# Graph network, sort and counts: bucket counts by summed signs, destination degrees counted inside the steps, half of the flag scatters behind the sort

## The reference

```python
h = relu(layernorm(x))
for _ in range(4):                     # STEPS
    msg = einsum('eij,ej->ei', (attr @ W_bond + b_bond).reshape(-1, 32, 32), h[dst])
    agg = segment_sum(msg, src)
    h = gru_cell(agg, h)
x = x + h
h = relu(layernorm(x))
deg = segment_sum(ones, dst)           # how many edges each node receives
dis = where(deg > 0, rsqrt(deg), 0)
out = x + segment_sum(h[src] * dis[src] * weight * dis[dst], dst)
```

## Time and profile before

| | us |
|---|---|
| median of 3 runs | 27753.59 (27752.26 to 27754.51) |
| the profiled execution, whole | 27758.91 |
| its span in the profile | 27757.1 |
| counting | 50 to 732 |
| placement | 757 to 4832 |
| layout | 4832 to 4876 |
| the four steps | 4876 to 22680 |

### The profile page before, as it was taken

The page is one execution under the profiler, slowest core; times in us unless marked ns, Lnnn a source line. Parts: engine busy times, 40 slices in busy tenths (PEclk is TensorE's granted clock), DMA queues, the critical chain, the costliest instruction groups (busy, mean ns, idle before and its releaser), DMA issues. The chain is left out here.

```text
span 27757.1 us, 248614 instructions
## 1 busy us (share of the span) xinstructions
PE 12374.2 (45%) x67675; PEld 9367.5 (34%) x67676; DVE 9831.1 (35%) x17524; ACT 4931.9 (18%) x12149; POOL 19766.5 (71%) x20823
## 2 busy tenths in 40 slices
PE   5566665455555455555455555545555530000004
PEld 5344443333333333333333333333333320000004
DVE  9899998222222222222222222222222230000007
ACT  7333333111111111111111111111111110000004
POOL 0677777777777677777677777767777767777771
PEclk8777777777777677777677777767777765555555
DMA  4233332111111111111111111111111111121113
GB/s 168 84 94 94 94 94 79 30 29 28 28 28 29 26 29 28 28 29 28 26 28 28 28 29 28 27 27 28 29 28 28 28 33 45 44 46 44 44 42 90
DMA packets 1814377, 1246.48 MB, mean 45 GB/s; under 512 B 1182629, under 2 KB 1744754, under 8 KB 1789679
## 3 DMA queue, kind: packets, MB, share of 16 engines
q1 hardware_dynamic: 583936, 850.03, 10.1%
q0 software_dynamic: 666016, 324.92, 8.0%
q10 hardware_dynamic: 564300, 70.11, 1.7%
HBM read 957.69 MB, written 285.80 MB: 45 GB/s over the span
## 5 line engine op out<-in xcount | busy, mean ns | idle before, releaser
L1083 POOL DMA_INDIRECT h_rows<-h_table,rec x13680 | 12910.7, 944 | 4284.0 <-issue 4118.8
L1233 PE MATMUL outer<-a_masked,h_by_quarter 128*128 128x136 f32 x27360 | 5316.2, 370 | 8726.5 <-DVE h_by_quarter L1124 8726.5
L1233 PEld LDWEIGHTS outer<-a_masked,h_by_quarter 128*128 128x128 f32 x27360 | 5045.0, 272 | 9193.2 <-issue 9193.2
L1279 ACT COPY outer_sums<-outer 128x408 f32<-128x408 f32 x4560 | 2276.2, 499 | 14770.2 <-PE outer L1233 14271.9
L1124 DVE TENSOR_TENSOR h_by_quarter<-h_rows,gates 128x1920 f32<-128x1920 f32 x912 | 1964.6, 2154 | 7011.0 <-DMA h_rows<-h_table,rec 7011.0
L1510 POOL DMA_INDIRECT messages_by_bucket<-ms,ix x3420 | 3279.1, 959 | 1063.5 <-issue 1042.4
L855 POOL DMA_INDIRECT edges_by_node<-row,place x3125 | 2992.9, 958 | 952.8 <-issue 945.2
L1117 DVE TENSOR_TENSOR a_masked<-rec,gates 128x2040 f32<-128x2040 f32 x912 | 2071.0, 2271 | 4308.7 <-PE outer L1233 4288.1
L1209 PE MATMUL msg_psum<-outer_sums,w_bond_blocks 128*128 128x480 f32 x7752 | 3521.2, 601 | 0.0
L1209 PEld LDWEIGHTS msg_psum<-outer_sums,w_bond_blocks 128*128 128x128 f32 x7752 | 1583.2, 215 | 1400.5 <-issue 1400.5
L1492 PE MATMUL pgb<-ident_f,gsp_by_chunk_of_tile 128*120 128x128 f32 x228 | 61.6, 426 | 3848.1 <-DVE gsp_by_chunk_of_tile L1430 3848.1
(11 more groups left out here) (277 smaller groups left out, 12593.5 us busy)
## 6 DMA issues: line engine op xcount, KB each, us to landing
h_rows<-h_table,rec POOLq DMA_INDIRECT x13680, 2.4
key_row<-source_keys SPq DMA_DIRECT2D x125, 1600.0 KB
rec<-edges_by_node SPq DMA_DIRECT2D x1140, 157.5 KB, 2.2
low_key_row<-source_low_keys SPq DMA_DIRECT2D x126, 800.0 KB
carry_flags<-carry_flags SPq DMA_DIRECT2D x285, 240.0 KB
mr<-messages_by_bucket SPq DMA_DIRECT2D x220, 264.0 KB, 2.7
messages_by_bucket<-zeros SPq DMA_DIRECT2D x36, 1600.0 KB, 37.0
chunk_sums<-scan_t ACTq DMA_DIRECT2D x912, 60.0 KB
```

The lines of the kernel that those rows point to most:

```text
L1083: pool.indirect_dma_start(out=hb[j][:, u, :], out_offset=None, in_=ht, in_offset=bass.IndirectOffsetOnAxis(ap=rec[j][:, u, W_DST:W_DST + 1 ...
L1233: last = pe.matmul(pt[(j * NB + g) % RING][:, at:at + KC], hq[j % 2][:, u, :, :].rearrange("p q d -> p (q d)"), am[j % 2][:, u, :, :].rear ...
L1279: act.copy(ts[b][:, :, at:at + w].rearrange("p k (u c) -> p u k c", c=CPT), pt[(j * NB + g) % RING][:, 0:GPB * KC].rearrange("p (u k c) -> ...
```

## The change

- Counting: DVE builds only `oh_s` and `oh_hs`, with keys that ACT has copied twice over once for all iterations (`lo_s2`, `hi_s2`). PE makes one product for each tile. The destination bucket counts come from ACT: 97 passes over all 3125 high keys of a partition, each giving sign(hi - h + 0.5) and its sum over the row (`accum_out`). Half the difference of two neighbouring sums is the count of a bucket in a partition, and the plan sums over partitions as before.
- Steps: in each group from the third on (55 of 57, 220 in all) DVE copies 15 tiles of destination keys into PSUM (`take_dst`), builds their onehots (`onehots_of_dst`), PE multiplies them in 15 products into `px` (`count_dst`), and DVE adds the result to `node_d`, which is cleared ahead of the steps. The keys `lo_d`, `hi_d` stay in SBUF for that.
- Flags: 49 of the 98 flag scatters stay ahead of the placement, 49 go into the layout block, where the wait for all of them is too.

```diff
+JD = 15
...
+    CS = NGR - 2
+    KI = up(STEPS * CS * JD, J1) // J1
+    assert STEPS * CS * JD >= T1 and KI > IT1
...
+        lo_d = sb("lo_d", [P, KI, J1], BF16)
+        hi_d = sb("hi_d", [P, KI, J1], BF16)
...
+                lo_s2 = sb("lo_s_twice", [P, IT1, J1, 2], BF16)
+                hi_s2 = sb("hi_s_twice", [P, IT1, J1, 2], BF16)
+                signs = [sb(f"signs{k}", [P, IT1, J1], BF16) for k in range(4)]
+                above = sb("above_bucket", [P, P])
+                nsign = sb("sign_sums", [P, HB + 1])
...
-                    ch(dve.tensor_scalar(half_below[:], iota_f[:], -0.5, None, ALU.add))
+                    ch(dve.tensor_scalar(above[:], iota_f[:], -1.0, 0.5, ALU.mult, ALU.add))
+                    ch(dve.memset(nsign[:, 0:1], float(T1)))
+                    ch(dve.memset(nsign[:, HB:HB + 1], -float(T1)))
...
+                    dve.wait_ge(s_key, 1)
+
                     def build(it, b, i):
                         dve.wait_ge(s_cnt, it + 1)
-                        dve.wait_ge(s_key, it + 1)
-                        for k, out_ in enumerate((oh_s, oh_hs, oh_d)):
-                            onehots(dve, out_[b][:], iota_b, key_v[b][:, k])
-                        last = onehots(dve, oh_hd[b][:], iota_b, key_v[b][:, 3, 0:JV])
-                        last.then_inc(s_oh_v, 1)
+                        onehots(dve, oh_s[b][:], iota_b, lo_s2[:, bass.ds(it, 1)].rearrange("p a u k -> p (a u) k"))
+                        onehots(dve, oh_hs[b][:], iota_b, hi_s2[:, bass.ds(it, 1)].rearrange("p a u k -> p (a u) k")).then_inc(s_oh_v, 1)
                     pairs(dve, IT1, build)
                     dve.wait_ge(s_cnt, IT1 + 2)
                     ch(dve.tensor_copy(node_s[:, 0:HB], pnode_s[:, 0:HB]))
-                    ch(dve.tensor_copy(ncode[:], pcode_d[:, 0:HB + 1]))
-                    ch(dve.tensor_tensor(node_d[:, 0:HB], ncode[:, 1:HB + 1], ncode[:, 0:HB], ALU.subtract))
-                    ch(dve.scalar_tensor_tensor(out=node_d[:, 0:HB], in0=node_d[:, 0:HB], scalar=0.5, in1=pnode_d[:, 0:HB],
-                                                op0=ALU.mult, op1=ALU.add))
+                    dve.wait_ge(s_sign, HB - 1)
+                    ch(dve.tensor_tensor(node_d[:, 0:HB], nsign[:, 0:HB], nsign[:, 1:HB + 1], ALU.subtract))
+                    ch(dve.tensor_scalar(node_d[:, 0:HB], node_d[:, 0:HB], 0.5, None, ALU.mult))
...
+                    act.wait_ge(s_split, 1)
+                    act.copy(lo_s2[:], lo_s[:, 0:IT1].unsqueeze(3).broadcast_to([P, IT1, J1, 2]))
+                    act.copy(hi_s2[:], hi_s[:, 0:IT1].unsqueeze(3).broadcast_to([P, IT1, J1, 2])).then_inc(s_key, 1)
                     act.wait_ge(s_split, 2)
-
-                    def build(it, b, i):
-                        act.wait_ge(s_cnt, it + 1)
-                        for k, key in enumerate((lo_s, hi_s, lo_d, hi_d)):
-                            last = act.copy(key_v[b][:, k], twice(of(key, it)))
-                        last.then_inc(s_key, 1)
-                        act.mul(neg[b][:], of(hi_d, it), -1.0).then_inc(s_neg, 1)
-                        act.wait_ge(s_neg, it + 1)
-                        for u in range(JC):
-                            last = act.activation(code_hd[b][:, u, :], half_below[:, 0:HB + 1], ACT.Sign, bias=neg[b][:, JV + u:JV + u + 1], scale=1.0)
-                        last.then_inc(s_code, 1)
-                    pairs(act, IT1, build)
+                    for h in range(1, HB):
+                        if h > 4:
+                            act.wait_ge(s_sign, h - 4)
+                        act.activation(signs[h % 4][:], hi_d[:, 0:IT1], ACT.Sign, bias=above[:, h:h + 1], scale=1.0,
+                                       accum_out=nsign[:, h:h + 1]).then_inc(s_sign, 1)
...
                     def count(it, b, i):
                         pe.wait_ge(s_oh_v, it + 1)
-                        pe.wait_ge(s_code, it + 1)
                         for u in range(J1):
-                            pe.matmul(pnode_s[:, 0:HB], oh_s[b][:, u, :], oh_hs[b][:, u, :], start=False, stop=False, skip_group_check=True)
-                            if u < JV:
-                                pe.matmul(pnode_d[:, 0:HB], oh_d[b][:, u, :], oh_hd[b][:, u, :], start=False, stop=False, skip_group_check=True)
-                            else:
-                                last = pe.matmul(pcode_d[:, 0:HB + 1], oh_d[b][:, u, :], code_hd[b][:, u - JV, :], start=False, stop=False,
-                                                 skip_group_check=True)
+                            last = pe.matmul(pnode_s[:, 0:HB], oh_s[b][:, u, :], oh_hs[b][:, u, :], start=False, stop=False, skip_group_check=True)
                         last.then_inc(s_cnt, 1)
...
-                    for h in range(HB):
-                        pool.indirect_dma_start(
-                            out=flags, out_offset=bass.IndirectOffsetOnAxis(ap=flag_at[:, h:h + 1], axis=0),
-                            in_=zrow[:], in_offset=None, bounds_check=NCH - 1, oob_is_err=False).then_inc(s_flag, 16)
+                    def clear_flags(columns):
+                        for h in columns:
+                            pool.indirect_dma_start(
+                                out=flags, out_offset=bass.IndirectOffsetOnAxis(ap=flag_at[:, h:h + 1], axis=0),
+                                in_=zrow[:], in_offset=None, bounds_check=NCH - 1, oob_is_err=False).then_inc(s_flag, 16)
+                    clear_flags(range(HB // 2))
...
-                    pool.wait_ge(s_flag, 16 * HB)
...
+                @block.gpsimd
+                def _(pool):
+                    for h in range(HB // 2, HB):
+                        pool.indirect_dma_start(
+                            out=flags, out_offset=bass.IndirectOffsetOnAxis(ap=flag_at[:, h:h + 1], axis=0),
+                            in_=zrow[:], in_offset=None, bounds_check=NCH - 1, oob_is_err=False).then_inc(s_flag, 16)
+                    pool.wait_ge(s_flag, 16 * HB)
...
+                dst_ps = pg[:, GB, CPT + NQ:CPT + NQ + 2 * JD]
+                o_dl = sb("dst_low_onehots", [P, JD, P], BF16)
+                o_dh = sb("dst_bucket_onehots", [P, JD, HB], BF16)
+                lo_all = lo_d[:].rearrange("p i u -> p (i u)")
+                hi_all = hi_d[:].rearrange("p i u -> p (i u)")
...
+                        def take_dst(g):
+                            tiles = bass.ds(s * (CS * JD) + (g - 2) * JD, JD)
+                            dve.wait_ge(s_do, s * CS + g - 1)
+                            dve.tensor_copy(dst_ps[:, 0:JD], lo_all[:, tiles])
+                            dve.tensor_copy(dst_ps[:, JD:2 * JD], hi_all[:, tiles]).then_inc(s_dk, 1)
+
+                        def onehots_of_dst(g):
+                            dve.wait_ge(s_dk, s * CS + g - 1)
+                            dve.wait_ge(s_dc, s * CS + g - 1)
+                            dve.tensor_tensor(o_dl[:], iota_b[:].unsqueeze(1).broadcast_to([P, JD, P]),
+                                              dst_ps[:, 0:JD].unsqueeze(2).broadcast_to([P, JD, P]), ALU.is_equal)
+                            dve.tensor_tensor(o_dh[:], iota_b[:, 0:HB].unsqueeze(1).broadcast_to([P, JD, HB]),
+                                              dst_ps[:, JD:2 * JD].unsqueeze(2).broadcast_to([P, JD, HB]), ALU.is_equal).then_inc(s_do, 1)
+
+                        def add_degrees(g):
+                            dve.wait_ge(s_dc, s * CS + g)
+                            dve.wait_ge(s_dd, s * CS + g - 1)
+                            dve.tensor_tensor(node_d[:, 0:HB], node_d[:, 0:HB], px[:, 0, 0:HB], ALU.add).then_inc(s_dd, 1)
+
                         def group(n0, ng, b, i, g, past, last=False):
                             if past == 2:
                                 scan(ng - 2, b, s * USES[b] + i - 1)
+                                take_dst(g)
                             for j in range(GI):
                                 if j + 1 < GI:
                                     make_a(n0 + j + 1, ng, j + 1, (j + 1) % 2)
+                                if past == 2 and j == 2:
+                                    add_degrees(g)
                                 spread_h(n0 + j, ng, j)
+                                if past == 2 and j == 0:
+                                    onehots_of_dst(g)
...
+                        def count_dst(ng, g_):
+                            pe.wait_ge(s_do, s * CS + g_)
+                            pe.wait_ge(s_sc, ng + 1)
+                            hold(pe)
+                            for u in range(JD):
+                                last = pe.matmul(px[:, 0, 0:HB], o_dl[:, u, :], o_dh[:, u, :], start=(u == 0), stop=(u == JD - 1))
+                            last.then_inc(s_dc, 1)
...
                                         weigh(ng - 1, 1 - b, n0 * NB + RING, j)
                                     if g == WEIGH_AT and j == 2 and past == 2:
```

(48 more changed lines are left out.)

2 lines of the change are left out of this document (removed).

## The result

| | us |
|---|---|
| before, median of 4 runs | 27754.05 |
| changed, median of 4 runs | 27436.11 (27435.28 to 27437.25) |
| ratio | 0.9886, 95% interval 0.9868 to 0.9903 |
| difference | -317.9; forecast -320.6 (27433) |

The account below looks back on a forecast made before the run. DVE was taken to bound the counting, POOL everything from placement to messages. Terms -294.6 - 57.3 + 32.0 + 0.2 = -319.7 us gave 27439.2 profiled, forecast 27433 us, range 27415 to 27500.

Parts of the forecast that it names:

- The counting: Counting block: DVE keeps only two onehots, 3.09 us an iteration in place of 5.45; ends at 437.7, -294.6 us.
- The rival that register addresses halve DVE's pace: Counting block: onehots reading keys at a register address take 6.3 us an iteration, +404, 27837 us; chance 0.03.
- that of ACT as the bound: Counting block: ACT's passes at 5.8 us each would set its end, 27608 us in all; chance 0.03.
- The flags ahead: Ahead of the placement: 49 flag scatters instead of 98 bring the first row scatter to 825.5, -57.3 us.
- Places first, flags second: Placement's start: with 49 flags POOL is through at 820.2, before the first places; the first row scatter goes at 825.5.
- The layout block: Layout block: 49 flags make POOL its bound, lasting 76.3 us in place of 44.3, +32.0 us.
- the meeting: Layout block: flag scatters held beside DVE's three wide products and a few copies, taken as +10 us.
- The steps: Steps: 990 us of added DVE work and 15 PE products a group hide beside POOL's gathers, cost 0.
- The slack itself: Steps: gather 9 after a group's second tile has 2.95 us to spare after three PE batches; the count takes 1.2.
- Sum: Whole kernel: -294.6 - 57.3 + 32.0 + 0.2 = -319.7 us; profiled 27758.9 becomes 27439.2, less 5.3 gives 27433.

Follow-up runs that it names:

- three and four times: Changed kernel with each group's 15 degree products made three times: 33908.20 us; four times: 34195.23 (kernel before 33510.48), again 34164.88 (before 33477.75).

## Why the prediction was right

**The counting, -294.6 forecast, -295.0 measured.** The mechanism held, and the sizes nearly: start 50.16 (50.0), 3.08 us an iteration over all 125 (3.09), 2.31 us behind the last onehot (1.7), end 437.5 (437.7). The last two erred by 1 us and 0.6 against each other. ACT's pass is 2.89 us and 0.19 for the sum, started 2.88 us apart (3.05 taken), so it ends at 329 and not at 346, which costs nothing. The rival that register addresses halve DVE's pace is out (1.83 us for 3200 elements, as before), and so is that of ACT as the bound.

**The flags ahead, -57.3 forecast, -56.8 measured.** The places were ready 67.6 us behind the first flag, as before; the first row scatter came 0.8 us after them, where I had taken 0.2. Places first, flags second was the right order on this chip; the runs on another show that it is this chip's: there the places move with the flags.

**The layout block, +32.0 forecast, +34.0 measured.** The meeting was sized right: the first scatter starts at 4480.28 and the last at 4551.25, 70.97 us for 48 distances of 1.275 = 61.2, so 9.8 us for the meeting against 10 taken. That it fits so well is in part luck. I had three products hold POOL for about 3.3 us each; the square took only 2.2 us from it, since the scatter beside it began 1.1 us late, and the third took 4.3, since its scatter was held by the `tensor_scalar` behind the product too, of which I had not thought. What was mis-sized is the ends: 0.7 us until POOL starts, and 5.7 us behind the last scatter where I took 3.8 from the end of the placement; why it is longer here is open.

**The steps, 0 forecast, -2.4 measured.** 969 us of DVE work where I had 990, the count at 1.23 us where I had 1.2, gathers at the same pace. The clearing of `node_d` took 0.17 us. Here the prediction is borne out by the pace and by first gather to last, and not by an experiment that reached the edge. The slack itself, in the tile that answers to the earlier trace rows, gather 9 last:

```profile
9653.38 1.72 PE L1276 MATMUL outer<-a_masked,h_by_quarter 128*128 128x136 f32 x6 [8.95 <-DVE h_by_quarter L1131]
9654.89 1.43 PE L1250 MATMUL scan_t_psum<-dst_bucket_onehots,dst_low_onehots 128*128 128x98 bf16 x15
9656.12 2.32 PE L1276 MATMUL outer<-a_masked,h_by_quarter 128*128 128x136 f32 x12
...
9660.94 0.94 POOL L1087 DMA_INDIRECT h_rows<-h_table,rec  x1 [0.30 <-issue]
```

The batches were done at 9658.44 and POOL was free at 9660.64, so 2.2 us are left, where 2.95 - 1.2 would be 1.75. With the count in between the stretch lasts 5.06 us in place of 4.44, 0.6 more for 1.23 us of products, because the third batch ran at a granted clock of 1.00, the upper level (2.4 GHz), and took 0.7 us, where the same batch took 1.4 at 0.50 before. In eleven groups that I read it lasts 4.9 to 5.7 us, so this help is not the same everywhere.

**Sum.** -319.7 against -318.4 up to the steps' start, and -3.1 behind. The parts erred by 0.4, 0.5 and 2 us; the sum is near because no wait took the place of the one removed. The two profiled spans differ by 321.6 us and the medians by 317.9, as the profiled execution stood 4.9 us above its median before and 1.1 after; and 27439.2 - 5.3 is 27433.9, which the forecast gives as 27433. So the last 3 us of the agreement mean nothing.

## What to carry to other kernels

Where one engine issues without a pause and all others wait for it, price a change by what it does to that engine's queue: work moved off a block that another engine bounds (here 295 us of onehots) is a full gain if it can be put beside the paced queue, and it costs nothing there as long as the tightest wait of that queue keeps its slack, which is read from the start of one named instruction. A queue's idle block is no free place beyond its length: 49 scatters of 1.275 us in a block of 44 us made it 78. And before a slack of 2 or 3 us is built on, remember that another chip may not have it.

## What the runs showed that I had not expected

- PE's clock. With half the products in the counting block the granted clock is 0.50 throughout it, the lower level (1.2 GHz), where it was 0.80 before; a product takes 283 ns in place of 240 or so. Products overlap, so what counts is the busy time of each: 272.04 / 3062 = 0.089 us where it was 398.78 / 6250 = 0.064. It costs nothing, because 25 products, 2.2 us, fit into DVE's 3.09 us at that level too. Here is PE's busy time first, and the granted clock third from the end:

```profile
50.00:430.00 380.00, 272.04 (x3062) 246.06 (x3063) 379.83 (x247) 279.49 (x194) 0.00 (x0) 0.50 0.68 286
```

- Three chips on which the same kernel takes 20% more, with engines standing for nothing that the profile names, while the counting block and the durations of nearly all instructions are the same (the message scatters of `c8` take 1.06 us on average with 98 flags ahead there, and 0.96 on the chip of the change).
- Code repeated in place is not the same as work repeated. With 60 products in a row on such a chip the first 36 came at full pace and later ones with gaps:

```profile
15070.35 2.93 PE L1250 MATMUL scan_t_psum<-dst_bucket_onehots,dst_low_onehots 128*128 128x98 bf16 x36
15074.06 0.20 PE L1250 MATMUL scan_t_psum<-dst_bucket_onehots,dst_low_onehots 128*128 128x98 bf16 x1 [0.77 <-issue]
15075.45 0.20 PE L1250 MATMUL scan_t_psum<-dst_bucket_onehots,dst_low_onehots 128*128 128x98 bf16 x1 [1.20 <-issue]
...
15078.99 1.74 PE L1250 MATMUL scan_t_psum<-dst_bucket_onehots,dst_low_onehots 128*128 128x98 bf16 x19 [0.44 <-issue]
```

10.4 us for what takes 4.9 at the pace of the first ones (15 in 1.23), so much of what "three and four times" cost is this and not the products. With 45 the gaps begin behind the 39th.
